# Bias of an attention's maxima on 64x64 tiles, and the turned scores' bias seeded in PSUM by ScalarE

## The reference

```python
scores = jnp.einsum('bhnqd,bhnkd->bhnqk', qw, kw) * scale + pos_bias[None, :, None]
probs = jax.nn.softmax(scores, axis=-1)
ow = jnp.einsum('bhnqk,bhnkd->bhnqd', probs, vw)
```

## Time and profile before

| | |
|---|---|
| median of 3 runs | 740.96 us (737.52, 740.96, 741.58) |
| the profiled execution | 740.13 us, of it the span 738.4 |
| PE (matmul) busy | 637.5 us, 86% |
| DVE busy | 514.3 us, 70% |
| ScalarE (ACT) busy | 371.0 us, 50% |
| POOL busy | 431.5 us, 58% |
| mean granted TensorE clock | 0.951 |

### The profile page before, as it was taken

How to read it: one execution, slowest core, us unless ns; L and a number is a source line. 1 busy time by engine, 2 the same in 40 slices (tenths; PEclk the granted TensorE clock), 3 DMA queues, 4 the chain that set the end, 5 groups by cost and what they waited for, 6 DMA issues and landing times.

```text
span 738.4 us, 33034 instructions
## 1 busy us (share of the span) xinstructions
PE 637.5 (86%) x13242; PEld 493.3 (67%) x13242; DVE 514.3 (70%) x1624; ACT 371.0 (50%) x546; POOL 431.5 (58%) x482
## 2 busy tenths in 40 slices
PE   3779999999999999999999999889999999995000
PEld 1346667666667666666666666679999999995000
DVE  6835776776787687777777767857886776664185
ACT  2133444444444544544444434467677777773076
POOL 7720435645546546646546555577777777777454
PEclk9989999999999999999999999999999999999555
DMA  6895337436355455465374451134335443331494
GB/s 160 243 272 148 120 95 190 135 103 187 111 136 157 129 156 149 122 169 148 103 190 130 111 173 33 29 101 139 102 111 159 110 106 111 104 99 51 158 404 153
DMA packets 83575, 103.53 MB, mean 140 GB/s; under 512 B 15488, under 2 KB 70144, under 8 KB 83424
## 3 DMA queue, kind: packets, MB, share of 16 engines
q1 hardware_dynamic: 71040, 73.87, 35.8%
q0 software_dynamic: 8640, 17.84, 7.6%
q10 hardware_dynamic: 3744, 9.70, 3.5%
HBM read 60.12 MB, written 40.79 MB: 137 GB/s over the span
## 4 chain that ended last, share of the span: by engine, by line
PE 64%; DVE 9%; DMA 7%; issue 6%; SPq 6%; POOL 4%; ACT 2%; ACTq 1%; DVEq 0%; POOLq 0%
PE o_ps L1339 5%; PE score_ps L1293 5%; PE o_ps L1463 4%; PE ctx_ps L1463 4%; PE ctx_ps L1353 4%; PE scoret_ps L1299 4%; SPq L278 4%; PE scoret_ps L1316 3%; PE o_ps L1333 3%; PE score_ps L1283 3%; DMA blocks<-scratch 3%; PE bank L1210 3%; DMA scratch<-qk_hl 2%; PE scoret_ps L1283 2%; PE score_ps L1450 2%
## 5 line engine op out<-in xcount | busy, mean ns | idle before, releaser
L295 POOL DMA_INDIRECT slots<-rows_sb,slot_at x128 | 127.5, 996 | 132.1 <-PE o_ps L1339 84.5
L831 DVE TENSOR_REDUCE neg_max<-score_ps 128x16 f32<-128x1024 f32 x109 | 133.3, 1223 | 84.6 <-PE score_ps L1283 83.0
L710 ACT ACTIVATE prob<-scoret_ps 128x1024 f32<-128x1024 f32 x109 | 111.6, 1024 | 133.2 <-PE scoret_ps L1283 130.4
L560 POOL DMA_INDIRECT results<-scaled_sb,result_at x142 | 136.4, 961 | 43.1 <-issue 35.2
L743 ACT CAST w_slot<-wgu_sb 128x1024 fp32r x71 | 74.6, 1051 | 0.2
L1339 PE MATMUL o_ps<-v_sb,prob 128*64 128x18 f32 x2048 | 70.1, 210 | 2.8 <-issue 2.8
L1293 PE MATMUL score_ps<-bias_hl,fold 128*128 128x512 f16 x218 | 66.8, 389 | 3.2 <-DVE neg_max L831 3.2
L1339 PEld LDWEIGHTS o_ps<-v_sb,prob 128*64 128x64 f32 x2048 | 66.4, 138 | 3.5 <-issue 3.3
L1299 PE MATMUL scoret_ps<-bias_hl,fold 128*128 128x512 f16 x218 | 66.1, 385 | 0.2 <-ACT prob L710 0.2
L689 ACT COPY v_sb<-bank 64x512 f32<-64x512 f32 (+1 forms) x64 | 36.0, 563 | 52.4 <-PE bank L1271 31.9
L1353 PE MATMUL ctx_ps<-diag,o_sb 128*64 128x64 f32 x896 | 52.2, 234 | 10.2 <-DVE o_sb L846 5.0
(11 more groups left out here) (186 smaller groups left out, 1528.8 us busy)
## 6 DMA issues: line engine op xcount, KB each, us to landing
stack<-scratch SPq DMA_DIRECT2D x32, 512.0 KB
blocks<-scratch SPq DMA_DIRECT2D x126, 128.0 KB
scratch<-qk_hl SPq DMA_DIRECT2D x120, 128.0 KB
xin<-slots SPq DMA_DIRECT2D x71, 130.0 KB, 2.3
blocks<-results ACTq DMA_DIRECT2D x16, 512.0 KB, 10.1
x_sb<-in_x SPq DMA_DIRECT2D x16, 256.0 KB
out<-y_sb SPq DMA_DIRECT2D x16, 256.0 KB, 3.0
results<-scaled_sb,result_at POOLq DMA_INDIRECT x142
```

Of the source, the lines that this page charges most:

```text
L295: nc.gpsimd.indirect_dma_start(slots, bass.IndirectOffsetOnAxis(ap=slot_at[:, k % 2, n:n + 1], axis=0), rows_sb[:, k % 2, n // TT, n % TT, ...
L560: pool.indirect_dma_start(results, bass.IndirectOffsetOnAxis(ap=result_at[s % RBUF][:, t:t + 1], axis=0), scaled_sb[:, s % RBUF, t, :], No ...
L710: act.activation(prob[:, (par + u) % 2, :], turned_scores(i, u)[:, :, :].rearrange("p b c -> p (b c)"), ACT.Exp).then_inc(exp_done, 1)
L831: dve.tensor_reduce(neg_max[:, par, :, v, :], ps[:, :, :].rearrange("p b (h k) -> p b h k", k=W), AX_X, ALU.max, negate=True).then_inc(max ...
```

## The change

`bias_s` takes only the high float16 part of the bias, which now lies in both halves of the partitions, and does so with four matmuls on 64x64 tiles instead of two on 128x128. The turned bias is kept in float32 in a tile of its own, `bias_f`. ScalarE copies it into `scoret_ps` behind each exponential, for the unit that comes next, waiting for its own `exp_done` first; PE waits for `seeded` ahead of `scores_t` and adds onto what is there. The first unit of pass 0 and all of pass 15 still go through `bias_t`. At the start DVE casts the two biases in two pieces and subtracts for the turned one alone.

```diff
--- before.py
+++ after.py
@@ -110,6 +110,7 @@
         b_q, b_k, b_v, b_qs = (sb(n, [P, 1]) for n in ("b_q", "b_k", "b_v", "b_qs"))
         b_o = sb("b_o", [P, P])
         bias_hl = sb("bias_hl", [P, 2, 1024], F16)
+        bias_f = sb("bias_f", [P, 1024])
 
 
         wgu_sb = sb("wgu_sb", [P, E, 2, 2 * HID])
@@ -228,6 +229,7 @@
         rows_cleared = sem("rows_cleared")
         s_ready, max_done = sem("s_ready"), sem("max_done")
         maxt_ps, maxt_ready, rows_in = sem("maxt_ps"), sem("maxt_ready"), sem("rows_in")
+        seeded = sem("seeded")
         st_ready, exp_done, pv_done = sem("st_ready"), sem("exp_done"), sem("pv_done")
         recip_done, norm_done = sem("recip_done"), sem("norm_done")
         ctx_done, ctxt_ready, wo_ps = sem("ctx_done"), sem("ctxt_ready"), sem("wo_ps")
@@ -302,6 +304,10 @@
         def turned_scores(i, u):
 
             return scoret_ps if there(i + 1) or u % 2 == 0 else score_ps
+
+        def by_scalar(i, u):
+
+            return (i, u) != (0, 0) and i < STEPS - 1
 
         def turned_ps(s):
 
@@ -339,9 +345,9 @@
                 sp.dma_start(b_v[:, :], bv.rearrange("(p a) -> p a", a=1)).then_inc(consts_in, 16)
                 sp.dma_start(b_o[:, :], bo.rearrange("(a d) -> a d", a=1).to_broadcast([P, DM])).then_inc(consts_in, 16)
                 sp.dma_start(rw_sb[:, :], rw_t).then_inc(rw_in, 16)
-                for n, src in ((0, bias), (1, bias_t)):
+                for tile, src in ((prob[:, 0, :], bias), (bias_f[:, :], bias_t)):
                     for rows in (0, 64):
-                        sp.dma_start(prob[rows:rows + 64, n, :], src).then_inc(bias_in, 16)
+                        sp.dma_start(tile[rows:rows + 64, :], src).then_inc(bias_in, 16)
 
                 def halves_out(k, par):
 
@@ -709,6 +715,10 @@
                         after(act, pv_done, NU * i + u - 1)
                         act.activation(prob[:, (par + u) % 2, :], turned_scores(i, u)[:, :, :].rearrange("p b c -> p (b c)"),
                                        ACT.Exp).then_inc(exp_done, 1)
+                        after_this = (i, u + 1) if u + 1 < NU else (i + 1, 0)
+                        if by_scalar(*after_this):
+                            act.wait_ge(exp_done, NU * i + u + 1)
+                            act.copy(scoret_ps[:, :, :].rearrange("p b c -> p (b c)"), bias_f[:, :]).then_inc(seeded, 1)
                         if u == 0 and there(i + 2):
                             xt_copy(i + 2, par)
                         if u == 1 and there(i + 2):
@@ -820,9 +830,10 @@
                 dve.wait_ge(halves, 3)
                 dve.tensor_tensor(qk_hl[:, 1, 1, :], qk_f[:, 1, :], qk_hl[:, 1, 0, :], ALU.subtract).then_inc(halves, 1)
                 dve.wait_ge(bias_in, 64)
-                dve.tensor_copy(bias_hl[:, :, :], prob[:, :, :]).then_inc(dve_made, 1)
-                dve.wait_ge(dve_made, 1)
-                dve.tensor_tensor(bias_hl[64:128, :, :], prob[64:128, :, :], bias_hl[64:128, :, :],
+                for n, tile in ((0, prob[:, 0, :]), (1, bias_f[:, :])):
+                    dve.tensor_copy(bias_hl[:, n, :], tile).then_inc(dve_made, 1)
+                dve.wait_ge(dve_made, 2)
+                dve.tensor_tensor(bias_hl[64:128, 1, :], bias_f[64:128, :], bias_hl[64:128, 1, :],
                                   ALU.subtract).then_inc(dve_made, 1)
                 clear(1)
 
@@ -1289,9 +1300,11 @@
                 def bias_s(k, v, ps=score_ps, behind=0):
 
                     after(pe, max_done, NU * k + v - behind)
-                    for n in range(2):
-                        pe.matmul(ps[:, n, :], fold[:, :], bias_hl[:, 0, n * 512:n * 512 + 512],
-                                  start=True, stop=False, skip_group_check=True)
+                    for a in range(2):
+                        for n in range(2):
+                            pe.matmul(ps[64 * a:64 * a + 64, n, :], fold[64 * n:64 * n + 64, 64 * a:64 * a + 64],
+                                      bias_hl[64 * n:64 * n + 64, 0, n * 512:n * 512 + 512],
+                                      start=True, stop=False, skip_group_check=True)
 
                 def bias_t(i, u):
                     after(pe, exp_done, NU * i + u - (0 if there(i + 1) or u == 0 else 1))
@@ -1310,6 +1323,8 @@
                     if u == 0:
                         pe.wait_ge(t_stacked, 80 * (i + 1))
                         pe.wait_ge(rows_in, 32 * (i + 1))
+                    if by_scalar(i, u):
+                        pe.wait_ge(seeded, NU * i + u)
                     for n in range(2):
                         for a in range(2):
                             rows = slice(64 * a, 64 * a + 64)
@@ -1378,7 +1393,7 @@
                     for u in range(TURNS):
                         if u < NU:
 
-                            if u or first:
+                            if (u or first) and not by_scalar(i, u):
                                 bias_t(i, u)
                             v = u if first else u + 1
                             if there(i + 1) and v < NU:
@@ -1400,7 +1415,7 @@
                         if u == NU and there(i + 2):
                             scores(i + 2, par, 0)
                         if u == NU + 1:
-                            if there(i + 1):
+                            if there(i + 1) and not by_scalar(i + 1, 0):
                                 bias_t(i + 1, 0)
                         if u == NU and last:
                             turn(0)
@@ -1472,7 +1487,7 @@
                 pe.wait_ge(rw_in, 16)
                 project_v(0, 0, 0)
                 project_v(0, 0, 1)
-                pe.wait_ge(dve_made, 2)
+                pe.wait_ge(dve_made, 3)
                 for v in range(NU):
 
                     bias_s(0, v, (score_ps, scoret_ps)[v % 2], 1)
```

## The result

The changed kernel took 770.17 us (median of four runs, 760.32 to 776.66), the kernel before 741.27 in the same comparison: a ratio of 1.030, 95% interval 1.024 to 1.035. (A ratio compares the faster executions of each kernel, those within 1.5% of its fastest; by the medians this one is 1.039.) The forecast was 734, with a range from 726 to 749. The execution that was profiled is the slowest of the four, 776.66 us; the mean granted clock of the four was 0.859, 0.859, 0.870 and 0.871, the two slower ones with the lower clock.

What follows compares the result with a forecast made beforehand. Bound: the loop of q copy, split, stores and loads, PE almost as slow. From 740.1 us: start 1.1, pass 0 1.2, passes 1 to 13 8, pass 14 0.7 less, half clock 5 more: 734, range 726 to 749.

Steps and rivals of the forecast that it cites:

- ScalarE's part of the loop: Exponential, seed, q copy: the q copy starts 0.27 us earlier a pass, held up by the seed of unit 2.
- self-wait: On ScalarE ahead of each seed, waiting for its own exponential: 0.1 us, beside 1.04 us for the seed.
- The distance of two units: Exponential, wait, seed, semaphore, maxima product in a row: no unit follows its predecessor by less than 2.95 us.
- The tiles: Maxima's bias as four 64x64 matmuls: 0.25 us, saving 0.3 or 0.2 us, 7 times a pass.
- Rival (d): In the maxima's bias the four tiles do not overlap, or ScalarE's write holds up PE's: near 745 us, chance 0.03.
- Rival (a): PE was the bound after all: 672 us, or about 705 with passes of 26 us; chance 0.07.
- The DMA part: Split, eight stores, five loads and their landings behind the q copy: untouched by the change.
- I expect it in a third of the passes: 5 us: Half clock at the head of a pass, after the wait for `blocks`: about 1.4 us a fall, 5 us in all.
- Rival (b): The clock falls in every pass: 13 falls at 1.4 us, 18 us instead of 5, 747 us; chance 0.22.
- by that rule every pass would pay: The skill's warning on loops that wait for a DMA each turn: each turn starts cold, so every pass pays.

Runs made afterwards that it cites:

- x4_bare: The changed kernel without the seed and its waits, the turned bias of passes 0 to 14 left out of the computation: 772.76 us, ratio 1.043.
- z3_fill7: The changed kernel plus six overwritten 128x128 products in turn 7 alone: 753.12 us, ratio 1.014.
- z2_bare_fill: The changed kernel without seed or turned bias in passes 0 to 14, plus two overwritten 128x128 products ahead of each maxima unit's four tiles: 754.48 us, ratio 1.016.
- w4_both_tiles: Against the kernel before: both biases on PE on 64x64 tiles, high float16 parts only, no seed on ScalarE: 739.49 us, ratio 0.993.
- v1_both_late: Against the kernel before: both biases on PE on 64x64 tiles, high parts only, DVE's copy of the rows behind turn 2's maxima: 731.04 us, ratio 0.980.
- x1_tiles: Against the kernel before: only the maxima's bias on 64x64 tiles, turned bias still on PE: 738.19 us, ratio 0.985; repeated 737.48 us, ratio 0.994.

## Why the prediction was wrong

**The bound of the kernel before was read rightly, and ScalarE's part of the loop moved much as the working said.** Take the head of pass 12, counted from the scores at 383.29 (in the working: from 352.51):

```profile
387.06 1.03 ACT L716 ACTIVATE prob<-scoret_ps 128x1024 f32<-128x1024 f32 x1
388.11 1.02 ACT L721 COPY scoret_ps<-bias_f 128x1024 f32<-128x1024 f32 x1
389.06 0.58 ACT L679 COPY xt_sb<-bank 128x512 f32<-128x512 f32 x1
389.87 1.02 ACT L716 ACTIVATE prob<-scoret_ps 128x1024 f32<-128x1024 f32 x1 [0.22 <-PE scoret_ps L1294]
390.92 1.02 ACT L721 COPY scoret_ps<-bias_f 128x1024 f32<-128x1024 f32 x1
392.17 0.69 ACT L686 ACTIVATE qk_f<-bank,b_qs 128x512 f32<-128x512 f32 x1 [0.23 <-PE bank L1221]
```

Exponential 0 starts 3.77 us behind these scores; I had 3.78. The q copy starts 8.88 behind; I had 8.92, and before it was 9.19. That this one fits is partly luck: I had the copy held up by the seed, and here it waits 0.23 us for PE, whose q projection starts 7.71 behind the scores where I had 7.51. The seed took 1.017 instead of 1.04 and no 0.1 us of self-wait. The Trainium skill's rule that ScalarE writes PSUM faster than SBUF (ScalarE: Activation LUTs, Step-by-step) agrees with this row in sign, as far as two different operations can be compared: 1017 ns for the copy into PSUM, 1051 for the cast of the same size into SBUF. The distance of two units was 2.81 us at its least, not 2.95.

**The tiles** took 0.24 us for the four (386.15 to 386.39), as taken from L1316:

```profile
386.15 0.41 PE L1305 MATMUL score_ps<-bias_hl,fold 64*64 64x512 f16 x4
386.39 0.39 PE L1331 MATMUL scoret_ps<-max_rows,half 64*64 64x512 bf16 x4
```

Rival (d) is out. Rival (a) is out as well: `x4_bare` has no turned bias at all and its passes at the full clock are 26.1 us or more, not 24, with PE busy 23.1 us of them. In the changed kernel the full-clock passes of 26.6 and 27.1 us come near the 26 of (a), but PE is busy only 23.7 us in each, so PE's work alone isn't what holds them.

**A full-clock pass was put too long.** I had 27.8 to 28.4; the profile has 27.08 here and 26.62 in the other. The DMA part, which I called untouched, was shorter: from the first store (367.87) to the scores (383.29) 15.4 us against 16.7 in the pass of the earlier trace rows, with SP's eight stores issued in 5.12 us. The error is on the good side and doesn't explain the result.

**The bound moved, and not where I had it.** I expected PE to stand before `scores(i + 2, 0)` for 1.5 to 2.4 us in most passes, waiting for `blocks`. In the pass from 367.87 it doesn't wait there at all:

```profile
383.29 0.42 PE L1294 MATMUL score_ps<-blocks,stack 64*64 64x128 f16 x16
```

and the chain, followed back through the pass, runs over DVE's normalised rows and maxima and over PE, with no store or load in it (start us, us, what):

```profile
365.48 2.41 DVE rows_sb L884 x4
...
368.55 1.22 DVE neg_max L842
369.82 0.41 PE score_ps L1305 x4
...
383.36 0.53 PE score_ps L1294 x16
```

The other full-clock pass shows the same. In the passes PE's waits for `blocks` of over 1 us are three: 2.8, 3.9 and 1.2 us, each of them just ahead of a fall or inside one.

**The step that failed is the clock.** I wrote "I expect it in a third of the passes: 5 us", at 1.4 us a fall. The profile has 16 falls and some 147 us at half clock, which cost some 54 us by the estimate below. Three things in the term were wrong:
- *The number.* I looked for idle time at one place, ahead of the wait for `blocks`. The changed kernel has its waits at three more: for DVE's maxima (16.1 us), for `o_sb` (12.9 us) and for the seed (9.3 us). I had costed DVE at nothing beyond the end of the pass, though the trace of the kernel before has 2.8 us of `norm` work just ahead of the maxima of turn 3; with PE earlier, DVE is late next:

```profile
361.84 1.41 DVE L873 TENSOR_SCALAR rows_sb<-res,mean_var,rstd 128x128 f32<-128x128 f32 x4
363.28 1.41 DVE L877 COPY rows_sb<-rows_sb 128x512 f32<-128x512 f32 x1
```

- *The size.* I priced a fall of 3.4 us at 1.4. Of the 16, six last 3.41 us and five 13.65, the others 6.83 to 23.89. The two passes with one fall of 13.65 take 31.8 and 32.1 us, some 5 more than at the full clock; the two that hold one of 3.41 besides take 33.8 and 33.9.
- *What keeps the clock.* I counted gaps only. The matmuls that the change takes away were part of what kept PE busy, and `z3_fill7` and `z2_bare_fill` show that putting useless ones back wins time.

Rival (b), at a chance of 0.22, had the right mechanism, but a price that was too low and mostly the wrong place. With 54 us over 16 falls, 3.4 each, its 13 falls would have given 734 - 5 + 44 = 773 us, near the result. The page that I named beside it (the Trainium skill, TensorE: Matmul & The Clock Gate, HAM oscillation) describes a kernel that starts each turn cold behind a DMA wait. Its waits are longer than the gaps that I forecast, so "by that rule every pass would pay" stretched it. Here ten of twelve passes pay, but for other reasons: of the 16 falls between 40 and 530 us only three come in or right behind a wait for `blocks` (of 1.0 to 3.9 us). Four follow waits of 2.0 to 2.1 us for DVE's maxima, and two come with waits of 0.9 and 1.5 us for the seed. One stands in pass 0 behind 2.4 us of idle time, and six have no idle time of over 1.03 us in the 4 us ahead.

**The sum in hindsight**, an estimate from the profiled executions: 13 passes at 27.1 instead of 28.44 would have given 17 us. The changed kernel is 36.5 us slower (776.66 against 740.13), so the low clock cost about 54, out of some 147 us spent at it, if all passes would otherwise have run like the two at the full clock. At half speed PE alone would lose up to 73; I take the rest as hidden behind waits for DMAs and DVE.

**What stays open.** Which amount of idle time or missing work brings the clock down isn't settled: `w4_both_tiles` keeps it with 20 us of waits for DVE, `z2_bare_fill` loses it at times with hardly any. Whether the seed's chain costs anything by itself at the full clock was not separated from the clock in a kernel that keeps it. Nor is it separated how much of the change's loss is DVE's wait as such: `v1_both_late` shows that this wait can cost over 1% with the clock nearly full.

## What to carry to other kernels

Before taking work from a TensorE that is nearly always busy (96% of the passes here) in a loop with another bound, ask what the granted clock will do once it waits: a pass at 27 us with a full clock is worth nothing if most hold falls and take 28 to 34. The test is cheap: put overwritten products where the engine will wait, and if more work is faster, the clock is what is lost. Then shorten the waits rather than the work: here a DVE copy moved by one turn was worth about as much as the fill, and in `v1_both_late` it made a gain of its own.

## What the runs showed of the hardware that I had not expected

- The granted clock, once down, stayed there for 3.41 to 23.89 us; in the 13.65 us from 348.29 PE was busy 12.89, so a busy engine isn't enough to bring it back at once.
- Leaving out work made a kernel slower by 4% (`x4_bare`), and 48 us of useless matmuls then took some 2.5% off (`z2_bare_fill`).
- ScalarE's float32 copy of 1024 columns from SBUF into PSUM took 1.017 us in 104 units, and matmuls with `start=False` added onto it.
- DVE's four row operations of L884 took 2.40 and 2.70 us in two passes of the changed kernel, for work that took 1.41 before in the same passes; over the whole run one takes 550 ns against 438. In `x1_tiles`, which has no loss, it takes 555, so this alone doesn't make the loss. What makes them long wasn't tried.
- On one chip the kernel before took 836 us instead of 741.
